# In the last round VectorE multiplies the experts' hidden values by the spread weights straight from PSUM

## The reference

```python
q, k, v = split_heads(x @ Wq), split_heads(x @ Wk), split_heads(x @ Wv)
attn = softmax(einsum('bhqd,bhkd->bhqk', q, k) * e ** -0.5) + bias
out = norm(einsum('bhqk,bhkd->bhqd', attn, v)) * gamma + beta      # eps 1e-3
x1 = layernorm(x + out)
h = einsum('btd,pd->btp', x1, hasher_w)
vals, idx = top_k(einsum('btp,np->btn', h, keys), 4)
w = softmax(vals)
for k in range(4):                     # the four experts of a token
    proj = silu(einsum('btd,btdp->btp', x1, values_down[idx[..., k]]))
    out2 = out2 + einsum('btp,btpd->btd', proj, values_up[idx[..., k]]) * w[..., k:k + 1]
return layernorm(x1 + (x1 + out2 * scale))
```

## Time and profile before

| what | value |
|---|---|
| runs | 301.14, 300.7, 298.92 us; median 300.7 |
| the profiled execution | 301.16 us, of it 299.1 us span |
| granted TensorE clock | 0.994 |
| TensorE (PE) busy | 278.4 us, 93% |
| VectorE (DVE) busy | 235.5 us, 79% |
| ScalarE (ACT) busy | 197.6 us, 66% |
| GpSimd (POOL) busy | 130.9 us, 44% |
| chain that ended last | PE 68%, DVE 12%, DMA 6%, ACT 5%, POOL 4% |

### The profile page before, as it was taken

How to read it: one execution, slowest core, us unless ns; L and a number is a source line. 1 busy time by engine, 2 the same in 40 slices (tenths; PEclk the granted TensorE clock), 3 DMA queues, 4 the chain that set the end, 5 groups by cost and what they waited for, 6 DMA issues and landing times.

```text
span 299.1 us, 10998 instructions
## 1 busy us (share of the span) xinstructions
PE 278.4 (93%) x4660; PEld 146.7 (49%) x4661; DVE 235.5 (79%) x517; ACT 197.6 (66%) x390; POOL 130.9 (44%) x218
## 2 busy tenths in 40 slices
PE   4969999999999989999999999999999999889992
PEld 2644433444434344444557554445565645367482
DVE  4767899989989978987787799987977864148854
ACT  3652487867776668689864876889656689941620
POOL 8476133110115641137556312189365031885852
PEclk9997999999999999999999999999999999999999
DMA  5565095264051202000403030006100000010011
GB/s 158 154 179 150 9 182 118 40 178 118 2 136 31 79 4 83 4 2 25 139 6 81 4 83 5 1 3 177 24 4 2 6 3 3 2 37 2 2 37 35
DMA packets 18574, 17.27 MB, mean 58 GB/s; under 512 B 6830, under 2 KB 16222, under 8 KB 18526
## 3 DMA queue, kind: packets, MB, share of 16 engines
q1 hardware_dynamic: 17856, 16.39, 21.6%
q10 hardware_dynamic: 670, 0.19, 0.3%
HBM read 12.18 MB, written 4.23 MB: 55 GB/s over the span
## 4 chain that ended last, share of the span: by engine, by line
PE 68%; DVE 12%; DMA 6%; ACT 5%; POOL 4%; issue 3%; SPq 1%; POOLq 0%; DVEq 0%
PE sm_ps L1256 16%; PE st_ps L1256 14%; PE ov_ps L1311 14%; PE mi_ps L1256 6%; PE si_ps L1256 5%; DVE neg_max L947 5%; DMA k_stack<-parts_dram 3%; ACT probs L801 2%; DMA wq_sb<-L_attn_Wq 2%; ACT w_rows L703 1%; PE si_ps L1336 1%; PE mi_ps L1318 1%; PE st_ps L1568 1%; PE sm_ps L1336 1%; PE st_ps L1442 1%
## 5 line engine op out<-in xcount | busy, mean ns | idle before, releaser
L947 DVE TENSOR_REDUCE neg_max<-sm_ps 128x1 f32<-128x512 f32 x256 | 166.4, 685 | 29.2 <-PE sm_ps L1256 24.9
L801 ACT ACTIVATE probs<-st_ps 128x512 f32<-128x512 f32 x256 | 138.2, 610 | 34.0 <-PE st_ps L1256 34.0
L1256 PE MATMUL sm_ps<-k_stack,q_stack 96*32 96x512 bf16 x984 | 97.1, 383 | 3.0 <-DVE neg_max L947 2.1
L1256 PE MATMUL st_ps<-q_stack,k_stack 128*32 128x512 bf16 x1024 | 88.6, 380 | 0.2 <-ACT probs L801 0.2
L1311 PE MATMUL ov_ps<-probs,v_cur 128*32 128x256 f32 x1024 | 76.4, 378 | 0.0
L1256 PEld LDWEIGHTS sm_ps<-k_stack,q_stack 96*32 96x32 bf16 x984 | 26.3, 94 | 50.6 <-DVE neg_max L947 33.9
L533 POOL TENSOR_TENSOR hid<-hid,w_rows 128x512 f32<-128x512 f32 x27 | 34.1, 1278 | 30.7 <-ACT w_rows L703 30.7
L1311 PEld LDWEIGHTS ov_ps<-probs,v_cur 128*32 128x32 f32 x1024 | 31.6, 110 | 22.7 <-ACT probs L801 0.4
L1256 PEld LDWEIGHTS st_ps<-q_stack,k_stack 128*32 128x32 bf16 x1024 | 27.7, 96 | 28.3 <-ACT probs L801 9.1
L1010 DVE SCALAR_TENSOR_TENSOR hid<-tanh_sb,mi_ps 128x512 f32<-128x512 f32 x24 | 16.3, 681 | 15.0 <-ACT tanh_sb L838 15.0
L1256 PE MATMUL mi_ps<-x_t,down_sb 128*32 128x512 f32 x192 | 25.1, 592 | 0.0
(11 more groups left out here) (189 smaller groups left out, 301.2 us busy)
## 6 DMA issues: line engine op xcount, KB each, us to landing
q_stack<-parts_dram SPq DMA_DIRECT2D x16, 288.0 KB
k_stack<-parts_dram SPq DMA_DIRECT2D x48, 96.0 KB
parts_dram<-parts SPq DMA_DIRECT2D x24, 128.0 KB, 2.4
x_sb<-L_attn_x SPq DMA_DIRECT2D x4, 256.0 KB, 4.6
out<-y_out SPq DMA_DIRECT2D x3, 256.0 KB, 2.3
down_sb<-L_ffn_values_down SPq DMA_DIRECT2D x1, 512.0 KB, 5.7
up_sb<-L_ffn_values_up SPq DMA_DIRECT2D x1, 512.0 KB, 7.9
rel_win<-rel_dram SPq DMA_DIRECT2D x1, 256.0 KB, 2.7
```

The lines of the kernel that those rows point to most:

```text
L801: nc.scalar.activation(probs[:, u % 2, j, :], st_ps[:, score_bank(u * J + j), :], ACT.Exp, scale=SCORE_SCALE).then_inc(probs_ready, 1)
L947: nc.vector.tensor_reduce(neg_max[:, g % 2, col:col + 1], sm_ps[:, c % 2, :], AX.X, ALU.max, negate=True).then_inc(max_ready, 1)
L1256: i = nc.tensor.matmul(dst[n * TILE:(n + 1) * TILE], weights[:, n * TILE:(n + 1) * TILE], moving, **flags)
```

## The change

In the last round alone (`not more`):

- ScalarE's eight copies `w_rows[:, j] <- si_ps` are not made.
- Pool's eight `weigh` are not made. `late_norm` follows at once on `split_weights`.
- VectorE gets eight `weigh_spread`, each a `tensor_tensor` of `hid[:, j]` (SBUF) by `si_ps` (PSUM). Each waits for the hidden value and for `w{j}`, counts `weighed`, then waits for its own count and only then counts `side_done`, which frees `si_ps`.

TensorE's instructions and their waits are what they were.

```diff
+        LAST_WEIGHED = {(12, 1): 0, (12, 3): 1, (13, 1): 2, (13, 3): 3, (14, 1): 4, (14, 3): 5, (15, 0): 6, (15, 1): 7}
...
                 if experts:
                     split_weights(f)
-                    for j in range(SHIFT_AFTER):
-                        weigh(f, t, j)
+                    if more:
+                        for j in range(SHIFT_AFTER):
+                            weigh(f, t, j)
                 if attention:
...
-                    if experts:
+                    if experts and more:
                         for j in range(SHIFT_AFTER, FJ):
                             weigh(f, t, j)
                             if late and j == NORM_AFTER:
                                 late_norm(t - 2)
+                    elif late:
+                        late_norm(t - 2)
...
+                        elif name in SPREAD and not more:
+                            continue
...
+            def weigh_spread(t, j):
+
+                dve.wait_ge(hidden_made, hidden_count(t - 1, j))
+                dve.wait_ge(side_ready, job(t, f"w{j}", is_side))
+                nc.vector.tensor_tensor(hid[:, j], hid[:, j], si_ps[:], ALU.mult).then_inc(weighed, 1)
+                dve.wait_ge(weighed, hidden_count(t - 1, j))
+                dve.sem_inc(side_done, 1)
...
+                if t == B - 1 and at in LAST_WEIGHED:
+                    weigh_spread(t, LAST_WEIGHED[at])
                 if s == 0 and 8 <= u < 8 + FJ:
                     hidden(t, u - 8)
```

## The result

The changed kernel takes 299.33 us, median of 22 runs (297.28 to 301.96), against 301.3 us for the kernel before, median of 22 (298.92 to 302.96). The ratio is 0.9946, with a 95% interval of 0.9922 to 0.997: 0.5% faster, at least 0.3 and at most 0.8, which is 0.9 to 2.4 us. (The quotient of the two medians is 0.9935 and lies inside that interval.) The forecast was 1.44 us, or 0.48%.

What follows compares the result with a forecast made beforehand. The prediction took ScalarE's full queue in steps 12 to 15 of the last round to hold TensorE. 1.27 us there plus 0.17 in the tail gave 1.44, from 300.7 to 299.2 us, range 297.9 to 300.9.

Steps and rivals of the forecast that it cites:

- What binds steps 12 to 15: Last round: ScalarE is full, its copies behind exponentials hold TensorE; no more than 2.1 us can come back.
- The round trip R: TensorE to VectorE and back over si_ps: 1.25 us (1.19 to 1.34), four pairs 5.15 instead of 6.26 us.
- The rest of the steps: Steps 12 to 15 outside the pairs: nothing between pairs, 0.16 us from w7 to the last values product.
- It reaches the tail: At the transpose of o_sb: margins near half a us, so all of the 1.27 us gets there.
- L976: VectorE in the tail: its second instruction takes 0.42 us instead of 0.94 without Pool's product beside it.
- How much of it gets through: Tail: of L976's 0.5 us, 0.17 passes (bounds 0 and 0.17), TensorE's up products take the rest.
- Rival B: Longer round trip, R 1.5 us, or another wait in the tail: gain 0.4 us, 299.9 to 300.3; chance 0.22.
- Rival C: Slower: VectorE's queue holds si_ps longer, from R = 1.61 us; 301.7 us with Pool's product duration; chance 0.07.
- Rival D: More: steps 12 to 15 reach TensorE's floor, 2.1 us, and the tail passes 0.5; 298.1 us; chance 0.09.

Runs made afterwards that it cites:

- experiment 1: Changed kernel, but ScalarE's eight copies stay and free the bank, VectorE multiplies from SBUF, only Pool's products gone; ratio to before 0.9975.
- experiment 4: Changed kernel, but VectorE makes a second product from the bank, into w_rows, before it frees it; ratio to before 1.0064.
- experiment 5: Changed kernel, but VectorE's product itself counts side_done and frees the bank, the separate count being that of weighed; ratio to before 0.994.
- experiment 6: Changed kernel with w5 and w6 each one place later and w7 behind the last values product; ratio to before 0.993.
- experiment 2: Changed kernel, but Pool makes two unused products out of SBUF from the copy of o_sb on; ratio 0.9946.
- experiment 3: Changed kernel, but Pool makes three fills from the copy of o_sb on; 9.14 us from the transpose to the second half of x1t.
- experiment 7: experiment 6 with VectorE's places as in the changed kernel, w6's product ahead of the last hidden value; ratio to before 0.992, median 298.03 us.

## Why the prediction was right, point by point

The sign, the size (1.44 against 1.5 us by the stretches) and the places were right. But two terms were off, and that the sum came out is luck: the steps gave 0.2 us less than I had said and the tail 0.3 more. So is the nearness of the time, 299.33 us against 299.2: the median of before was 301.3 in 22 runs and not 300.7, and the difference of the two medians is 2.0 us.

- *What binds steps 12 to 15.* Right: ScalarE's queue ahead of the copy. Experiment 1 gives all of the gain there back when only the copies return, and experiment 4 shows that the round trip over the one bank is what TensorE waits for in the changed kernel. Not all of it was the bank, though. Before, the pair of `w6` and `w7` was stretched by the score product between them, which waited for an exponential and came 0.34 us behind `w6` and not 0.22 (the row is below the list); from there on TensorE had no more than its own work. That pair's 0.12 us and the 0.15 behind `w7` come from exponentials that no longer stand behind copies, the other 0.78 from the bank.
- *The round trip R.* I took 1.25 us from 1.19 to 1.34; it was 1.31 to 1.39 in the four pairs, at and beyond the upper end. In step 14 it is 0.54 from TensorE's start to VectorE's (259.13 to 259.67), 0.69 for the product, and 0.11 to TensorE's next product. The product was right. The term that was mis-sized is the way from TensorE to the reader: I took 0.44 from ScalarE, and VectorE needed 0.1 more (0.52 to 0.59 in the four pairs). The count cost 0.05 (experiment 5). The four pairs took 5.36 us and not 5.15.
- *The rest of the steps.* 0.15 for the last interval, against 0.16; nothing between the pairs. The steps gave 1.06 us and not 1.27, which is the lower bound that stood beside it.
- *It reaches the tail.* Right, with margins of 0.54 us for the hidden value and 0.37 for the eighth product; I had said near half a us. Experiment 6 shows what stands behind these margins.
- *L976.* 0.43 us, as forecast, and the cause is shown by experiments 2 and 3.
- *How much of it gets through.* This step was wrong. I let 0.17 us of the 0.5 pass, and 0.48 passed. TensorE was the second bound, as I had said, but it stood earlier. I took its place from the one profile that I had, where the sum of the up products ended 8.06 us behind the transpose, and said that TensorE's work ran there without a gap. The pause of 0.18 us in the loading of weights was in it; it is what splits the last 13 matmuls off in the earlier trace rows. In the changed kernel the sum ended 7.83 and 7.87 us behind the transpose. `late_y` could start at 7.87 and 7.91, and not at 8.11 as I had reckoned. It was still held, by 0.1 us or a little more: it came 0.64 and 0.68 us behind the first half of `x1`, where it takes 0.53 when nothing holds it (both profiles of before, and experiment 2). The rest is the last piece: I took 0.69 us from the start of `late_y` to the second half of `x1`, but behind a `late_y` that TensorE has held it is 0.61 (0.60 in experiment 3). With the pause, experiment 3 shows what would have got through: 9.14 us, 0.23 less than before. So 0.17 was too low even for the profile that I had, and 0.48 holds where there is no pause.
- *The chances.* The gain was within 1%, as I had said with 0.87. Rival B (little left) asked for R = 1.5; R stayed 0.1 to 0.2 away from it. Rival C needed R = 1.61, and with pairs of 1.91 to 2.02 it was there (experiment 4). Rival D's 2.1 us in the steps are out of the change's reach, because step 14 has no cover; with a cover (experiment 6) the steps gave 1.7, and then ScalarE's exponentials were in the way.

The weights of the score product between `w6` and `w7`, in the profile of before:

```profile
262.04 0.10 PEld L1256 LDWEIGHTS st_ps<-q_stack,k_stack 128*32 128x32 bf16 x4 [0.45 <-ACT probs L801]
```

## What to carry to other kernels

Where one PSUM bank passes between TensorE and a reader, count the round trip and the work that TensorE has between two uses of it. A reader with an empty queue is worth more than a fast one: VectorE's product takes 0.69 us and ScalarE's copy 0.60, but the copy stood behind exponentials. Below the covering work (here 1.30 us) nothing more is to be had. When the reader changes, look at what stands behind the new wait in its queue: the same two instructions of VectorE in the other order cost 0.7 us in experiment 6 against experiment 7. And take a bound that decides how much of a gain passes from more than one profile, or from the durations of its parts.

## What the runs showed of the hardware

The time up to `w0` of the last round differed by 4.6 us from profile to profile, in code that is the same in all kernels, and most of it goes with the mean granted clock between 16 and 32 us, in the opening ahead of the rounds. Twelve profiles:

| granted clock from 16 to 32 us | start of `w0` in us |
|---|---|
| 1.00 (4 profiles) | 249.58, 249.99, 250.57, 250.93 |
| 0.89 (4 profiles) | 251.44, 251.65, 251.78, 252.53 |
| 0.79 (4 profiles) | 252.93, 252.95, 254.12, 254.21 |

The changed kernel's two profiles show the two ends (busy times of PE, PEld, DVE, ACT and POOL with the instructions, then the clock), first the one at `w0` = 252.95:

```profile
18.00:20.00 2.00, 0.47 (x5) 0.24 (x3) 0.87 (x2) 1.23 (x3) 0.71 (x1) 1.00 0.76 180
22.00:24.00 2.00, 2.00 (x6) 1.48 (x7) 0.73 (x2) 0.20 (x1) 2.00 (x5) 0.50 0.76 197
24.00:26.00 2.00, 2.00 (x6) 1.18 (x6) 1.38 (x2) 0.00 (x0) 1.74 (x3) 0.50 0.77 186
```

and the one at 250.93:

```profile
22.00:24.00 2.00, 2.00 (x10) 1.48 (x11) 1.89 (x4) 0.20 (x1) 2.00 (x5) 1.00 0.78 193
24.00:26.00 2.00, 2.00 (x29) 1.14 (x31) 2.00 (x4) 1.02 (x1) 1.75 (x2) 1.00 0.78 197
```

In the first, TensorE is busy for only 0.47 of the 2 us from 18 to 20 and waits for a transfer of `k_stack` until 20.82. While it waits its granted clock falls to 0.50, the lower of its two levels, 1.2 GHz. From 22 to 26 us it gets through 12 matmuls instead of 39. In the second it had been as idle (0.50 of 2 us) and kept the full 2.4 GHz. In the profile of experiment 1 it did nothing at all from 18 to 20 us and kept it too. The 4.6 us between the ends are as large as the spread of the runs (4.0 us before, 4.7 after) and three times the effect of the change, which is why the change is read from stretches here. What decides between the two wasn't tried.

The other thing is the difference between Pool's reading and writing: a product of Pool beside a VectorE instruction with two operands in SBUF made that instruction take 1.14 us instead of 0.43, fills did nothing to it, and VectorE's products with one operand in PSUM took 0.69 us beside Pool's products (Pool multiplied there from 284.55 to 288.29).
